# A layer's tail: stored residual rows and two accumulating DMAs in place of loads, adds and stores

## What is computed

```
x = x + _L0_attn_ref(_layernorm(x, axis=-1), ...)     # the residual rows
x = x + _L0_ffn_ref(_layernorm(x, axis=-1), ...)
...
topk_probs, selected = jax.lax.top_k(probs, TOPK)      # TOPK = 2, 8 experts
capacity = max(1, math.ceil(CAP_FACTOR * A / NUM_EXPERTS))   # 640 slots for each expert
...
expert_out = jnp.einsum('ecd,ehd->ech', pre * jax.nn.silu(gate), ff_post_act_weight)
updates = eo_flat[dispatch] * kept_w.astype(x.dtype)[:, None]
out = jnp.zeros((T, DMODEL), x.dtype).at[st].add(updates)
```

## Time and profile before

| | us |
|---|---|
| median of 3 runs | 331.68 (331.42 to 332.87) |
| profiled execution | 332.46 |
| its span, first to last instruction | 330.6 |
| PE busy | 264.2 (80%) |
| DVE busy | 263.3 (80%) |
| POOL busy | 192.4 (58%) |
| ACT busy | 131.3 (40%) |
| mean granted clock of PE | 0.917 |

### The profile page before, as it was taken

The page is one execution under the profiler, slowest core; times in us unless marked ns, Lnnn a source line. Parts: engine busy times, 40 slices in busy tenths (PEclk is TensorE's granted clock), DMA queues, the critical chain, the costliest instruction groups (busy, mean ns, idle before and its releaser), DMA issues.

```text
span 330.6 us, 4799 instructions
## 1 busy us (share of the span) xinstructions
PE 264.2 (80%) x1432; PEld 188.6 (57%) x1432; DVE 263.3 (80%) x618; ACT 131.3 (40%) x270; POOL 192.4 (58%) x152
## 2 busy tenths in 40 slices
PE   5789999649749977976697258689999999999820
PEld 3335444225326433543446136579999999999810
DVE  1699599999999999999999889684887887555333
ACT  3175796305433443343311300143553554654410
POOL 1454926599747664656572502777567777772640
PEclk9996799759998997999899659999999999999985
DMA  8005002526940001000100200224243343320168
GB/s 233 8 1 127 0 2 66 125 45 153 284 167 21 0 0 31 0 0 0 32 0 0 86 12 8 51 48 122 73 127 101 100 145 93 108 80 26 45 187 230
DMA packets 23958, 24.28 MB, mean 73 GB/s; under 512 B 2752, under 2 KB 17408, under 8 KB 23936
## 3 DMA queue, kind: packets, MB, share of 16 engines
q1 hardware_dynamic: 18752, 17.53, 18.9%
q0 software_dynamic: 2560, 5.25, 6.1%
q10 hardware_dynamic: 2624, 1.24, 1.4%
HBM read 13.00 MB, written 6.82 MB: 60 GB/s over the span
## 4 chain that ended last, share of the span: by engine, by line
PE 44%; DVE 24%; issue 11%; POOL 8%; ACT 5%; DMA 5%; DVEq 1%; ACTq 1%; POOLq 0%; SPq 0%
PE psum L1544 11%; DVE ring L550 6%; PE psum L1523 5%; PE psum L1525 5%; PE psum L1524 5%; POOL ring L1177 5%; DVE psum L540 4%; PE psum L1370 3%; PE psum L1332 3%; PE psum L1286 2%; DMA small<-in_small 1%; PE psum L1276 1%; POOL parts L1162 1%; PE psum L1497 1%; DMA ring<-pairs 1%
## 5 line engine op out<-in xcount | busy, mean ns | idle before, releaser
L1177 POOL TENSOR_TENSOR ring<-ring,cbc 128x1024 f32<-128x1024 f32 x31 | 73.1, 2361 | 43.7 <-DVE ring L550 42.4
L1332 PE MATMUL psum<-stack,sel_r 128*128 (+1 forms) x120 | 50.8, 522 | 25.1 <-DVE ring L550 23.1
L1370 PE MATMUL psum<-ring,cst 128*128 128x512 f32 x128 | 66.4, 647 | 0.9 <-POOL ring L1177 0.9
L550 DVE TENSOR_TENSOR_SCAN ring<-ring,psum 128x1024 f32<-128x1024 f32 x25 | 57.1, 2285 | 1.6
L1231 POOL DMA_INDIRECT ring<-rows,gid x40 | 38.8, 971 | 31.3 <-issue 24.8
L982 ACT ACTIVATE ring<-psum,nega 128x510 f32<-128x510 f32 x64 | 40.4, 680 | 36.7 <-PE psum L1332 34.8
L1332 PEld LDWEIGHTS psum<-stack,sel_r 128*128 128x128 f32 x120 | 22.1, 201 | 51.2 <-DVE ring L550 23.5
L1241 POOL DMA_INDIRECT pairs<-ring,sid x40 | 40.1, 1004 | 18.8 <-issue 15.4
L859 DVE TENSOR_TENSOR ring<-psum,ring 128x320 f32<-128x320 f32 x64 | 31.3, 491 | 21.9 <-ACT ring L1088 17.0
L1088 ACT ACTIVATE ring<-psum 128x320 f32<-128x320 f32 x64 | 27.9, 437 | 38.0 <-PE psum L1525 38.0
L1523 PE MATMUL psum<-stack 128*128 128x320 f32 x128 | 40.9, 319 | 0.5 <-ACT ring L1088 0.5
(11 more groups left out here) (187 smaller groups left out, 357.1 us busy)
## 6 DMA issues: line engine op xcount, KB each, us to landing
stack<-parts SPq DMA_DIRECT2D x16, 256.0 KB, 3.8
pairs<-zero SPq DMA_DIRECT2D x1, 2048.0 KB, 12.3
win_s<-in_wg SPq DMA_DIRECT2D x8, 256.0 KB, 3.2
win_s<-in_w SPq DMA_DIRECT2D x8, 256.0 KB, 3.9
w_s<-in_w SPq DMA_DIRECT2D x8, 256.0 KB, 2.8
ring<-pairs SPq DMA_DIRECT2D x6, 256.0 KB, 4.1
xt<-in_x SPq DMA_DIRECT2D x4, 256.0 KB, 4.4
rows<-xn SPq DMA_DIRECT2D x4, 256.0 KB, 2.3
```

Source lines behind the costliest of these rows:

```text
L550: v.tensor_tensor_scan(hh[:, s].rearrange("p a b -> p (a b)"), da[:, s].rearrange("p a b -> p (a b)"), inputs.rearrange("p a b -> p (a b)" ...
L1177: g.tensor_tensor(hc[:, s], hh[:, s], cb, ALU.mult).then_inc(s_product, 1)
L1332: ins = mm(bank(to), sel, stack[:, half, kind, bass.ts(c, CH)], start=True, stop=True)
L1370: ins = mm(bank(YB), wred[:, o:o + D], hc[:, s, k, :], start=(grp == 0), stop=(grp == NG - 1))
```

## The change

The stores of the residual rows move from the tail to the scan: SP's queue stores chunk c of `xt` to `out` as soon as `s_x2` tells that it is final, ahead of the store of the same chunk's normalised rows. In the tail, no table comes back to the core. Pool issues one DMA for each table, from `pairs` in memory to `out` in memory, which adds instead of overwriting. Source and destination are seen as 128 rows of 8 KB (16 token rows in a row). The first is issued between the scatters of tiles 1 and 2 of the last expert, after waits for the stores of `out` and for the scatters of experts 0 to 6. The second waits for the last scatters and for the first addition, since both read and write all of `out`. The eight additions of DVE, the loads and stores of SP and ACT in the tail and the two buffers `back` are gone.

```
--- before
+++ after
...
@@ -227,8 +225,6 @@
         sg = later(2, HALF)
         hT = later(2, FC, CAP)
         ye = later(DEEP, NQ, D)
-
-        back = [later(NT, D), ring[:, GX0:GX0 + NT * D].rearrange("p (j d) -> p j d", d=D)]
         zero = sb("zero", [P, D])
 
 
@@ -327,8 +323,7 @@
         s_weighed = sem("s_weighed")
         s_scattered = [sem(f"s_scattered{b}") for b in range(DEEP)]
         s_cleared = sem("s_cleared")
-        s_back = [[sem(f"s_back{k}{c}") for c in range(NC)] for k in range(2)]
-        s_result = sem("s_result")
+        s_back = [sem(f"s_back{k}") for k in range(2)]
         s_x = [sem(f"s_x_chunk{c}") for c in range(NC)]
         s_stack = sem("s_stack")
         s_in_weights = [sem(f"s_in_weights{b}") for b in range(2)]
@@ -339,7 +334,8 @@
 
         xv = x.rearrange("(c j p) d -> c p j d", j=TPC, p=P)
         outv = out.rearrange("(c j p) d -> c p j d", j=TPC, p=P)
-        pairv = [pairs[k * T:(k + 1) * T, :].rearrange("(c j p) d -> c p j d", j=TPC, p=P) for k in range(2)]
+        pairv = [pairs[k * T:(k + 1) * T, :].rearrange("(r q) d -> r (q d)", r=P) for k in range(2)]
+        out_rows = out.rearrange("(r q) d -> r (q d)", r=P)
         rowv = rows.rearrange("(c j p) d -> c p j d", j=TPC, p=P)
 
         def bank(k, w=CH):
@@ -417,8 +413,12 @@
                 nc.sync.dma_start(w2_s[:, e, :, :], w2[e]).then_inc(s_out_weights[e], 16)
 
             with sp.Fori(0, NC - 1) as c:
+                sp.wait_ge(s_x2, c + 1)
+                nc.sync.dma_start(outv[c], xt[:, bass.ts(c, TPC), :]).then_inc(s_out_stored, 16)
                 sp.wait_ge(s_xn2, TPC * c + TPC)
                 nc.sync.dma_start(rowv[c], xn[:, 0:TPC, :]).then_inc(s_rows_stored, 16)
+            sp.wait_ge(s_x2, NC)
+            nc.sync.dma_start(outv[NC - 1], xt[:, TPC * (NC - 1):, :]).then_inc(s_out_stored, 16)
             sp.wait_ge(s_xn2, TPC * (NC - 1) + 1)
             sp.wait_ge(s_last_xn2, TPC - 1)
             nc.sync.dma_start(rowv[NC - 1], xn[:, 0:TPC, :]).then_inc(s_rows_stored, 16)
@@ -430,18 +430,10 @@
                     nc.sync.dma_start(win_s[:, b, 1, :], w1[2 * i + (2 + b)]).then_inc(s_in_weights[b], 16)
                     sp.wait_ge(s_down, 2 * i + (b + 1))
                     nc.sync.dma_start(w2_s[:, b, :, :], w2[2 * i + (2 + b)]).then_inc(s_out_weights[b], 16)
-            for b in range(DEEP):
-                sp.wait_ge(s_scattered[b], 16 * NQ * (E // DEEP if b < DEEP - 1 else E // DEEP - 1))
-            for c in range(NC):
-                nc.sync.dma_start(back[0][:, TPC * c:TPC * (c + 1), :], pairv[0][c]).then_inc(s_back[0][c], 16)
-            sp.wait_ge(s_scattered[DEEP - 1], 16 * NQ * (E // DEEP))
-            for c in range(0, NC, 2):
-                nc.sync.dma_start(back[1][:, TPC * c:TPC * (c + 1), :], pairv[1][c]).then_inc(s_back[1][c], 16)
-            for c in range(0, NC, 2):
-                sp.wait_ge(s_result, c + 1)
-                nc.sync.dma_start(outv[c], xt[:, TPC * c:TPC * (c + 1), :]).then_inc(s_out_stored, 16)
             sp.wait_ge(s_out_stored, 16 * NC)
             sp.wait_ge(s_rows_stored, 16 * NC)
+            sp.wait_ge(s_back[0], 16)
+            sp.wait_ge(s_back[1], 16)
 
 
         @blk.vector
@@ -889,17 +881,6 @@
             tokens_low(0, 0, (1,))
             for e in range(E):
                 expert(e, e % 2)
-            for k in range(2):
-                for c in range(NC):
-                    js = slice(TPC * c, TPC * (c + 1))
-                    dve.wait_ge(s_back[k][c], 16)
-                    if k:
-                        ch.until(lower[c])
-                        v.tensor_tensor(xt[:, js, :], xt[:, js, :], back[1][:, js, :], ALU.add).then_inc(s_result, 1)
-                    else:
-                        if c == 0:
-                            lower = []
-                        lower.append(ch.mark(v.tensor_tensor(xt[:, js, :], xt[:, js, :], back[0][:, js, :], ALU.add)))
 
 
         @blk.scalar
@@ -1120,12 +1101,6 @@
                 if e + 1 < E:
                     spread_tokens(e + 1, (e + 1) % 2)
             weigh_last(E - 1, range(2, NQ))
-            act.wait_ge(s_scattered[DEEP - 1], 16 * NQ * (E // DEEP))
-            for c in range(1, NC, 2):
-                nc.scalar.dma_start(back[1][:, TPC * c:TPC * (c + 1), :], pairv[1][c]).then_inc(s_back[1][c], 16)
-            for c in range(1, NC, 2):
-                act.wait_ge(s_result, c + 1)
-                nc.scalar.dma_start(outv[c], xt[:, TPC * c:TPC * (c + 1), :]).then_inc(s_out_stored, 16)
 
 
         @blk.gpsimd
@@ -1232,10 +1207,10 @@
                                          in_offset=bass.IndirectOffsetOnAxis(ap=gid[:, e, q:q + 1], axis=0)
                                          ).then_inc(s_gathered[e % DEEP][q], 16)
 
-            def scatter(e):
+            def scatter(e, tiles=range(NQ)):
 
                 pool.wait_ge(s_scatter_ids, 2 * e + 2)
-                for q in range(NQ):
+                for q in tiles:
                     pool.wait_ge(s_weighed, NQ * e + q + 1)
                     plain(pool)
                     g.indirect_dma_start(out=pairs, out_offset=bass.IndirectOffsetOnAxis(ap=sid[:, e, q:q + 1], axis=0),
@@ -1248,8 +1223,23 @@
             for e in range(E - DEEP):
                 scatter(e)
                 gather(e + DEEP)
-            for e in range(E - DEEP, E):
+            for e in range(E - DEEP, E - 1):
                 scatter(e)
+
+            def add_table(k):
+
+                g.dma_start(out=out_rows, in_=pairv[k], accum_op=ALU.add, max_dma_last_dim=8192
+                            ).then_inc(s_back[k], 16)
+
+            scatter(E - 1, range(2))
+            pool.wait_ge(s_out_stored, 16 * NC)
+            for b in range(DEEP):
+                pool.wait_ge(s_scattered[b], 16 * NQ * (E // DEEP) if b < DEEP - 1 else 16 * NQ * (E // DEEP - 1))
+            add_table(0)
+            scatter(E - 1, range(2, NQ))
+            pool.wait_ge(s_scattered[DEEP - 1], 16 * NQ * (E // DEEP))
+            pool.wait_ge(s_back[0], 16)
+            add_table(1)
 
 
         @blk.tensor
```

More of the change, by code:

```diff
@@ L218, in build @@
         kw = sb("kw", [P, E, NQ])
-        GX0 = taken[0]
         gx = later(DEEP, NQ, D)
-        assert DEEP * NQ >= NT
         stack_flat = stack[:].rearrange("p h k t -> p (h k t)")
```

## The result

The changed kernel took 338.38 us in the median of its first runs (335.9 to 339.92), the kernel before 332.2 beside it: a ratio of 1.018, interval 1.011 to 1.025. In a second, longer series of runs the medians were 338.1 and 332.97 us, with a ratio over all runs of 1.012 (1.007 to 1.018). It is slower, as forecast, and inside the range of 328.5 to 339.6. But it lost 6.2 and 5.1 us where 2.3 were forecast, and 338.38 lies above the 332.8 to 336.8 that the likeliest case had for its own. The runs of this kernel spread by some 4 us, with the granted clock; the length of the tail in the traces is steadier and carries most of what follows.

A forecast was written before the change was run, and what follows sets the result against it. Transfers were taken to bound the tail; first addition's start 315.1, two additions of 8.0 and 0.35, 0.7, 0.5 and 0.3 us gave 332.95 against 330.6, so a median of 334.0 us, range 328.5 to 339.6.

The forecast's parts named there:

- the likeliest case: Tail: each addition takes A from 7.4 to 9.4 us with scatters queued, giving 332.8 to 336.8 us; chance 0.42.
- What bounds the tail, and the early stores: Transfers bound the tail after the last scatters, some 10.5 us; the four new stores in the scan cost nothing.
- A = 8.0 us: Each addition's time from issue to landing: 2.0 start and finish, 5.6 for two reads, 0.35 for the last row.
- The order on Pool: Pool's first addition starts at 315.1 us behind tile 1 of the last expert, the remaining scatters at 316.7 to 319.3.
- the added 0.35 for a first use: Extra 0.35 us on the first addition, since the first scatter and Pool's first gather were slow.
- Scatters behind the addition, and the way to the second: Three scatters land 0.7 us after the first addition; Pool needs 0.5 us more to its second.
- The end, 0.3 us: From the second addition's landing to the span's end, 0.3 us stay as they are.
- One pass: Rival: reading and writing `out` ride along with the table's read, A = 5.1 us, 328.5 us in all; chance 0.16.
- Peak rate: Rival: two reads at 437 GB/s, A = 6.8 us, no change at 331.6 us; chance 0.22 with its skill variant.
- three passes: Rival: reads and write share the DMA engines, A = 10.8 us, clearly slower at 339.6 us; chance 0.15.
- held up by the first addition: Rival: Pool waits until the first addition has landed before its three scatters, 338.1 us; chance 0.05.

The follow-up runs named there:

- the copy: The changed kernel with its first adding DMA made a plain copy of the same 1 MB: 335.69 us, ratio 1.007 against the kernel before.

## Why the prediction was right, and where it was not

**The whole.** The direction was right, the size was not, and the clear verdict owes something to luck. The run with the drain in an idle time is the changed kernel nearly without the term that was overlooked: 334.77 us against the forecast 334.0, but with a ratio of 1.004, which by the prediction's own limit of 0.5% is no change. It was Pool's drain, not in the prediction, that made the change clearly slower.

**What bounds the tail, and the early stores.** Right. The new stores cost nothing that their own run could tell. The changed kernel's queue shows them where they were expected, with room behind each:

```profile
156.49 0.38 SPq L417 DMA_DIRECT2D out<-xt  x1
163.65 0.38 SPq L419 DMA_DIRECT2D rows<-xn  x1
179.58 0.40 SPq L421 DMA_DIRECT2D out<-xt  x1
183.13 0.39 SPq L424 DMA_DIRECT2D rows<-xn  x1
```

**A = 8.0 us.** Right: 8.14 and 8.1, and each counted once for each addition. Its parts hold as well. The model had two reads at the 372 GB/s of long rows, 0.35 for the last rows and 2.0 of start and finish. The engines worked for 5.9 us on an addition (model: 5.6 + 0.35), at 2.1 times a copy's time for each byte, which leaves 2.2 for start, finish and gaps. The parts were a guess by the nearest rows; the copy is what bears them out.

The Trainium skill's account (Collectives: The Full Stack, on the bandwidth ceiling) has an addition run at half the copying rate, since it reads twice. The trace agrees: 179 GB/s against 379 while the engines work. That page's figure of about 31 GB/s for each engine was not reached: 379 GB/s are 24 for each of the 16. The estimate from it, 4.2 us for the bytes, stands against 5.9 measured.

**The order on Pool.** Right. Relative to the start of the last 24 matmuls the first addition was expected after 2.1 us and started after 1.8; the added 0.35 for a first use is not to be seen, the row is 1.02 us long.

**Scatters behind the addition, and the way to the second.** 0.7 + 0.5 = 1.2 us expected, 0.84 measured. The three scatters did queue. The first of them, issued at 318.60, landed 6.9 us later instead of 2.2, just behind the addition's landing at 325.40. The last landed at 325.95, and 0.3 later the second addition started.

```profile
DMA to landing us min/median/max: 2.2/2.3/6.9
```

The Trainium skill's rule of ring order (DMA: Bandwidth & Descriptors, on queues, rings and completion order) agrees with that row, and the trace prices it: about 0.5 us behind the addition's landing, for 192 KB.

**The end, 0.3 us.** This is the term that was mis-sized. "0.3 us of the end stay as they are" took the end of SP's waiting for the end of the program. With Pool as the last engine the closing drain comes behind, and returns 3.4 us after the landing: 3.65 us from landing to end instead of 0.3. Sum of the differences: -0.3 (start), -0.2 (first addition), -0.35 (way to the second), +0.1 (second addition), +3.35 (end) = +2.6, and the expected 19.96 us from the matmuls' start to the end became 22.55. The first four terms together were 0.75 too high, the last one was 3.35 too low. The part of the profile that would have told it is the row of Pool's drain in L108, which was not read: 8572 ns, returning 5.4 us after the last landing, under cover of SP's and ACT's loads and stores. With this term the sum would have come to 5.7 us more than before, against the 5.0 of the traces.

**The rivals.** One pass would have been A = 5.1: even the plain copy needs 5.7. Peak rate (6.8, or 7.15 with the 0.35 that the prediction left out of this rival) and three passes (10.8) are out. Pool was not held up by the first addition: its next scatter starts at 318.60, 0.3 us after the addition's row ends. That this rival's time of 338.1 is nearly the measured one is chance.

## What to carry to other kernels

When an engine's list becomes the last to end, read its closing drain in the profile of before: what was hidden behind other queues becomes part of the time. A Pool list with some 80 DMAs had 3 to 5 us of it, and one drain in an idle stretch took 2.9 of 3.4 us away at no cost that the tail shows. And before a load, an addition on an engine and a store are replaced by one adding DMA, compare the two paths' landings: here 1 MB added in memory took 8.1 us on a path where load plus store took 10, and two of them in series, which can't overlap with anything, gave back more than the shorter path saved.

## What the runs showed that was not expected

- Pool's drain: 0.5, 2.4 and 3.4 us behind the last landing with 12, 57 and 82 DMAs of Pool since the last drain, where Pool's last issue ended some 7 us before the landing; 0.5, 1.1, 4.5 and 5.4 with 10, 25, 70 and 80, where it ended 1.3 us before.
- A copy of 1 MB from memory to memory by Pool's queue, in rows of 8 KB, lands after 5.7 us, of which the engines work 2.8: 379 GB/s while they work, 179 for an addition. With rows of 2 KB instead of 8 an addition took 0.2 to 0.6 us longer.
- An adding scatter of 128 rows of 512 bytes costs Pool 1.55 us of issue instead of 0.97, a direct adding DMA of 128 rows about 1.0 against 0.61 for the copy.
